# Banded attention with the query and key weights multiplied once

## The reference, cut to what matters

```python
x = x + attn(_layernorm(x))         # the banded attention, changed
x = x + xattn(_layernorm(x), ctx)   # 16 heads over 1601 context rows
x = x + ffn(_layernorm(x))          # 16 heads over itself, then 4 experts

def attn(x, W_qkv, b_qkv, ln_w, ln_b):
    q, k, v = split(x @ W_qkv + b_qkv, 3)
    scores = (q @ k.T) / sqrt(256 * 64)
    scores = scores * band_mask        # keys i-63 .. i, no softmax
    return layer_norm(scores @ v, ln_w, ln_b)
```

## Time and profile before

| | |
|---|---|
| median of 3 runs | 1580.51 us (1579.86 to 1581.3) |
| the profiled execution, its own time | 1582.69 us |
| its span | 1580.8 us |
| PE / DVE / ACT / POOL busy | 1505.1 / 1353.2 / 1256.3 / 192.1 us |
| share of the span | 95% / 86% / 79% / 12% |
| mean granted TensorE clock | 0.989 |

### The profile page before, as it was taken

The page is one execution under the profiler, slowest core; times in us unless marked ns, Lnnn a source line. Parts: engine busy times, 40 slices in busy tenths (PEclk is TensorE's granted clock), DMA queues, the critical chain, the costliest instruction groups (busy, mean ns, idle before and its releaser), DMA issues.

```text
span 1580.8 us, 35391 instructions
## 1 busy us (share of the span) xinstructions
PE 1505.1 (95%) x14142; PEld 626.5 (40%) x14142; DVE 1353.2 (86%) x1914; ACT 1256.3 (79%) x2434; POOL 192.1 (12%) x236
## 2 busy tenths in 40 slices
PE   7977999999999999988999999999999999999997
PEld 6865422222222222346422222222222222338997
DVE  4765999999999999545899999999999999686654
ACT  1136489999999999767469999999999999776654
POOL 3101520000000000000560000000000000003443
PEclk9999999999999999999989999999999999999999
DMA  7000000000000000000003000000000012112111
GB/s 180 0 24 19 1 1 2 2 2 2 2 2 2 2 1 2 2 1 2 0 2 121 2 2 2 2 2 1 2 2 2 2 46 63 28 41 77 56 51 37
DMA packets 34134, 31.19 MB, mean 20 GB/s; under 512 B 10812, under 2 KB 30846, under 8 KB 33982
## 3 DMA queue, kind: packets, MB, share of 16 engines
q1 hardware_dynamic: 31246, 21.99, 4.9%
q0 software_dynamic: 2736, 7.08, 1.5%
HBM read 22.63 MB, written 6.68 MB: 19 GB/s over the span
## 4 chain that ended last, share of the span: by engine, by line
PE 71%; DVE 20%; ACT 6%; issue 2%; DMA 0%; SPq 0%; POOLq 0%; DVEq 0%
PE bank L843 25%; PE bank L830 21%; DVE nm_part L955 15%; PE s_pair L1379 4%; PE bank L1404 4%; PE s_pair L816 4%; PE s_pair L188 2%; ACT p_arena L939 2%; PE s_pair L861 1%; PE bank L627 1%; PE bank L607 1%; ACT o_sb L922 1%; PE bank L869 1%; PE bank L178 1%; PE bank L191 1%
## 5 line engine op out<-in xcount | busy, mean ns | idle before, releaser
L939 ACT ACTIVATE p_arena<-bank 128x512 f32<-128x512 f32 (+1 forms) x1856 | 1003.5, 597 | 67.2 <-PE bank L830 44.8
L955 DVE TENSOR_REDUCE nm_part<-s_pair 128x2 f32<-128x1024 f32 x896 | 1024.6, 1209 | 31.0 <-PE s_pair L816 29.8
L843 PE MATMUL bank<-p_arena,v_aug 128*32 128x256 f32 (+1 forms) x7424 | 596.7, 393 | 13.9 <-ACT o_sb L922 11.7
L816 PE MATMUL s_pair<-x_and_k,q_arena 48*128 48x512 f16 (+1 forms) x2048 | 555.1, 359 | 8.0 <-DVE nm_part L955 6.2
L830 PE MATMUL bank<-q_arena,x_and_k 49*128 49x512 f16 (+1 forms) x1856 | 551.0, 385 | 0.9 <-ACT q_arena L662 0.7
L843 PEld LDWEIGHTS bank<-p_arena,v_aug 128*32 128x32 f32 (+1 forms) x7424 | 147.6, 108 | 387.4 <-ACT p_arena L939 347.6
L830 PEld LDWEIGHTS bank<-q_arena,x_and_k 49*128 49x128 f16 (+1 forms) x1856 | 110.5, 94 | 374.1 <-ACT p_arena L939 331.9
L1031 POOL TENSOR_TENSOR attn_tok<-turned_sums,rden 128x256 f32<-128x256 f32 x30 | 18.6, 620 | 1021.1 <-DVE rden L974 1021.1
L816 PEld LDWEIGHTS s_pair<-x_and_k,q_arena 48*128 48x128 f16 x2048 | 110.7, 94 | 37.2 <-DVE nm_part L955 25.1
L1379 PE MATMUL s_pair<-q_arena 128*128 128x128 f32 x608 | 71.3, 275 | 2.4 <-DVE src_sb L1066 1.8
L1379 PEld LDWEIGHTS s_pair<-q_arena 128*128 128x128 f32 x608 | 70.6, 192 | 3.7 <-DVE src_sb L1066 2.0
(11 more groups left out here) (288 smaller groups left out, 1162.6 us busy)
## 6 DMA issues: line engine op xcount, KB each, us to landing
q_arena<-nm_T SPq DMA_DIRECT2D x512, 0.2 KB
x_and_k<-in_L_ffn_W SPq DMA_DIRECT2D x4, 1024.0 KB, 5.0
v_aug<-in_L_ffn_W SPq DMA_DIRECT2D x8, 512.0 KB, 5.9
res_rows<-x_and_k SPq DMA_DIRECT2D x1, 2048.0 KB, 8.5
x_rows<-src_sb SPq DMA_DIRECT2D x4, 512.0 KB, 3.0
x_and_k<-in_x SPq DMA_DIRECT2D x1, 1536.0 KB, 10.6
p_arena<-in_ctx SPq DMA_DIRECT2D x12, 128.0 KB, 2.0
q_arena<-in_L_attn_W_qkv SPq DMA_DIRECT2D x1, 768.0 KB, 5.3
```

Source lines behind the costliest of these rows:

```text
L816: last = pe.matmul(m_tile[slot % 2][:, part * 512 + place:part * 512 + place + width], q_op[rows, pair, at_q:at_q + P], k_op[rows, pair, k ...
L843: last = pe.matmul(o_bank[32 * a:32 * a + 32, low:low + width], v_aug[0:m, kt, b % 4 * 4 + a, :], at.prob(4 * unit + i)[0:m, low:low + wid ...
L939: act.activation(at.prob(4 * unit + i)[0:m, :], score_bank[k % 3][0:m, :], ACT.Exp, scale=SCALE).then_inc(z["exp"], 1)
L955: dve.tensor_reduce(partials[:, first:second + 1:second - first], banks, AX.X, ALU.max, negate=True).then_inc(z["m_free"], 1)
```

## The change

The change computes Wq Wk^T once, ahead of the first tile, and puts it in the place of the query weights. Rows are then projected to keys alone, and their raw transposed form takes the place of the queries. The bias Wq bk is added to the keys, now by ScalarE in two activations of 128 columns. The term that comes from the query bias depends on the key row alone, so it is computed as a 257th column of the values and added to the scores as a per-row scalar while they are masked, in two operations of 128 columns. `band_v` moves to `p_arena` and grows to 257 columns; `xT` goes. The semaphores `ld_small` and `kept` are merged into `ld_rows` and `res_bias`, so VectorE's wait ahead of the cross attention counts two more loads.

The fold itself (`fold_tensor`, `fold_scalar`, `fold_vector`): eight transposes of the two weight halves, their copies, four products of 256 columns, ten products of one column, and the copies back. TensorE waits for all of it (`fold` at 9) before it turns the first tile.

```diff
-        band_v = carve(q_arena, 3584, 4, C)
+        band_v = carve(p_arena, 512, 4, C + 1)
-        band_rows = carve(q_arena, 7168, 3, C)
+        v_row = q_arena[:, 7168:7168 + C + 1]
+        band_rows = carve(q_arena, 7168 + C + 1, 2, C)
-        xT = carve(p_arena, 512, 2, KC, P)
+        wq_T, wk_T, bq_wide = attn_tok[:, 0:KC, :], attn_tok[:, KC:2 * KC, :], carve(attn_tok[:, 4, :], 0, KC, P)
+        key_bias = attn_tok[:, 5, 0:KC]
...
+        def fold_tensor(pe):
+            pe.wait_ge(s["ld_band"], 16 * 5)
+            for half, b in ((0, 2), (1, 3)):
+                for o in range(KC):
+                    for k in range(KC):
+                        last = pe.transpose(bank(b)[:, o * C + k * P:o * C + (k + 1) * P],
+                                            w_band[:, k, half * C + o * P:half * C + (o + 1) * P], ident[:, :])
+            last.then_inc(s["fold"], 1)
+            pe.wait_ge(s["fold"], 4)
+            pe.wait_ge(s["ld_band"], 16 * 5)
+            for m in range(KC):
+                for o in range(KC):
+                    pe.matmul(bank(4)[:, m * C:(m + 1) * C], wk_T[:, o, m * P:(m + 1) * P], wq_T[:, o, :], start=o == 0, stop=o == KC - 1)
+            for m in range(KC):
+                for o in range(KC):
+                    pe.matmul(bank(5)[:, m:m + 1], wq_T[:, o, m * P:(m + 1) * P], bqk_col[:, KC + o:KC + o + 1], start=o == 0, stop=o == KC - 1)
+            for m in range(KC):
+                for o in range(KC):
+                    pe.matmul(bank(5)[:, KC + m:KC + m + 1], wk_T[:, o, m * P:(m + 1) * P], bqk_col[:, o:o + 1], start=o == 0, stop=o == KC - 1)
+            for o in range(KC):
+                last = pe.matmul(bank(5)[:, 2 * KC:2 * KC + 1], bq_wide[:, o, :], bqk_col[:, KC + o:KC + o + 1], start=o == 0, stop=o == KC - 1)
+            last.then_inc(s["fold"], 1)
+
+        def fold_scalar(act):
+            act.wait_ge(s["fold"], 1)
+            act.activation(wq_T, bank(2).rearrange("p (o c) -> p o c", o=KC), ACT.Copy).then_inc(s["fold"], 1)
+            act.wait_ge(s["fold"], 5)
+            act.activation(w_band[:, :, 0:C], bank(4).rearrange("p (m c) -> p m c", m=KC), ACT.Copy).then_inc(s["fold"], 1)
+
+        def fold_vector(dve):
+            dve.wait_ge(s["fold"], 1)
+            dve.wait_ge(s["ld_band"], 16 * 5)
+            dve.tensor_copy(bq_wide, bqk_col[:, 0:KC].unsqueeze(2).broadcast_to([P, KC, P])).then_inc(s["fold"], 1)
+            dve.tensor_copy(wk_T, bank(3).rearrange("p (o c) -> p o c", o=KC)).then_inc(s["fold"], 1)
+            dve.wait_ge(s["fold"], 5)
+            dve.tensor_copy(key_bias, bank(5)[:, 0:KC]).then_inc(s["fold"], 1)
+            dve.tensor_copy(w_band[:, :, 2 * C - 1:2 * C].rearrange("p k u -> p (k u)"), bank(5)[:, KC:2 * KC]).then_inc(s["fold"], 1)
+            dve.tensor_copy(v_row[:, 0:1], bank(5)[:, 2 * KC:2 * KC + 1]).then_inc(s["fold"], 1)
...
         def band_tensor(pe):
             pe.wait_ge(s["const"], 4)
-            pe.wait_ge(s["ld_band"], 16 * 5)
+            fold_tensor(pe)
             pe.wait_ge(s["band_zero"], 2)
+            pe.wait_ge(s["fold"], 9)
...
                     pe.wait_ge(s["band_st"], i + 1)
+                    pe.wait_ge(s["band_qkv"], i + 1)
...
-                    pe.wait_ge(s["band_qkv"], 2 * i + 2)
+                    pe.wait_ge(s["band_k"], i + 1)
...
-                    for f in range(4):
+                    q, x_T = (r - 1) % 2, band_qk[:, (r - 1) % 4, 0:KC, :]
+                    for f in range(KC):
...
-                        last = pe.matmul(bank(4 + q)[:, 0:C], xT[:, q, k, :], w_band[:, k, 2 * C:3 * C],
+                        last = pe.matmul(bank(4 + q)[:, 0:C + 1], x_T[:, k, :], w_band[:, k, 2 * C - 1:3 * C],
...
                     norm_root(act, r % 2, s["band_ln"], 4 * i, s["band_ln_root"])
+                    if isinstance(i, int) and i == 0:
+                        fold_scalar(act)
                     act.wait_ge(s["band_xT_ps"], i + 1)
-                    if some(i - 1):
-                        act.wait_ge(s["band_qkv_ps"], i - 1)
-                    act.activation(xT[:, r % 2, :, :], bank(r % 2)[:, 0:C].rearrange("p (k t) -> p k t", k=KC),
+                    act.activation(band_qk[:, r % 4, 0:KC, :], bank(r % 2)[:, 0:C].rearrange("p (k t) -> p k t", k=KC),
                                    ACT.Copy).then_inc(s["band_xT"], 1)
+
+                if (i := tile_at(t, 1, NT)) is not None:
+                    act.wait_ge(s["band_qkv_ps"], i + 1)
+                    if isinstance(i, int) and i == 0:
+                        act.wait_ge(s["fold"], 9)
+                    for f in range(KC):
+                        last = act.activation(band_qk[:, (r - 1) % 4, KC + f, :], bank(2 + (r - 1) % 2)[:, f * P:(f + 1) * P],
+                                              ACT.Identity, bias=key_bias[:, f:f + 1])
+                    last.then_inc(s["band_k"], 1)
...
-                    dve.tensor_tensor(band_st[:, (r - 2) % 2, :], bank(6)[:, 0:2 * P], band_mask[:, :],
-                                      ALU.mult).then_inc(s["band_st"], 1)
+                    dve.wait_ge(s["band_qkv"], i + 1)
+                    for h, keys in ((0, (r - 2) % 4), (1, (r - 3) % 4)):
+                        half = slice(h * P, (h + 1) * P)
+                        last = dve.scalar_tensor_tensor(band_st[:, (r - 2) % 2, half], bank(6)[:, half], band_v[:, keys, 0:1],
+                                                        band_mask[:, half], ALU.add, ALU.mult)
+                    last.then_inc(s["band_st"], 1)
...
                     norm_apply(dve, i, r % 2, x_sb[:, i, :], xin[:, r % 2, :], s["band_ln"], 4 * i, s["band_ln_root"])
+                    if isinstance(i, int) and i == 0:
+                        fold_vector(dve)
...
-                    dve.tensor_tensor(band_qk[:, q, :, :], bank(2 + q % 2).rearrange("p (f t) -> p f t", f=4),
-                                      bqk_col[:, :].unsqueeze(2).broadcast_to([P, 4, P]), ALU.add).then_inc(s["band_qkv"], 1)
-                    dve.tensor_tensor(band_v[:, q, :], bank(4 + q % 2)[:, 0:C], band_rows[:, 0, :],
-                                      ALU.add).then_inc(s["band_qkv"], 1)
+                    if isinstance(i, int) and i == 0:
+                        dve.wait_ge(s["fold"], 9)
+                    dve.tensor_tensor(band_v[:, q, :], bank(4 + q % 2)[:, 0:C + 1], v_row, ALU.add).then_inc(s["band_qkv"], 1)
...
-            dve.wait_ge(s["ld_rows"], 16 * len(ROWS))
+            dve.wait_ge(s["ld_rows"], 16 * (len(ROWS) + 2))
```

More of the change, by code:

```diff
@@ L108, in decoder_layer_kernel @@
                  "band_av", "band_out", "band_root", "band_ln_root", "band_xb", "xw_ps", "xw", "v_const", "k_const", "q_const",
-                 "ld_small", "res_bias", "kept")
+                 "res_bias", "band_k", "fold")
         x_view = io["x"][0].rearrange("(t p) c -> p t c", p=P)
@@ L167, in tick @@
                     q, prev = (r - 3) % 4, (r - 4) % 4
-                    pe.matmul(bank(7)[:, 0:C], band_st[:, q % 2, 0:P], band_v[:, q, :], start=True, stop=False)
-                    pe.matmul(bank(7)[:, 0:C], band_st[:, q % 2, P:2 * P], band_v[:, prev, :],
+                    pe.matmul(bank(7)[:, 0:C], band_st[:, q % 2, 0:P], band_v[:, q, 1:C + 1], start=True, stop=False)
+                    pe.matmul(bank(7)[:, 0:C], band_st[:, q % 2, P:2 * P], band_v[:, prev, 1:C + 1],
                               start=False, stop=True).then_inc(s["band_av"], 1)
                 if (i := tile_at(t, 2, NT)) is not None:
-                    pe.wait_ge(s["band_qkv"], 2 * i + 2)
+                    pe.wait_ge(s["band_k"], i + 1)
                     if some(i):
@@ L183, in tick @@
                     if some(i - 1):
-                        pe.wait_ge(s["band_qkv"], 2 * (i - 1))
-                    q = (r - 1) % 2
-                    for f in range(4):
+                        pe.wait_ge(s["band_k"], i - 1)
+                        pe.wait_ge(s["band_qkv"], i - 1)
+                    q, x_T = (r - 1) % 2, band_qk[:, (r - 1) % 4, 0:KC, :]
+                    for f in range(KC):
                         for k in range(KC):
-                            pe.matmul(bank(2 + q)[:, f * P:(f + 1) * P], w_band[:, k, f * P:(f + 1) * P], xT[:, q, k, :],
+                            pe.matmul(bank(2 + q)[:, f * P:(f + 1) * P], w_band[:, k, f * P:(f + 1) * P], x_T[:, k, :],
                                       start=k == 0, stop=k == KC - 1)
                     for k in range(KC):
-                        last = pe.matmul(bank(4 + q)[:, 0:C], xT[:, q, k, :], w_band[:, k, 2 * C:3 * C],
+                        last = pe.matmul(bank(4 + q)[:, 0:C + 1], x_T[:, k, :], w_band[:, k, 2 * C - 1:3 * C],
                                          start=k == 0, stop=k == KC - 1)
@@ L251, in tick @@
                     ring, c = 2 + q3, 5 * i
-                    dve.scalar_tensor_tensor(band_tmp[:, q3, :], o, mean_var[:, ring, 0:1], band_rows[:, 1, :],
```

(22 more changed lines are left out.)

## The result

The changed kernel takes 1590.62 us in the median of 6 runs (1589.09 to 1600.28), the kernel before 1579.75 us in the median of 6 (1579.03 to 1581.3). The ratio is 1.0069, 95% interval 1.0039 to 1.0098: slower by 10.9 us.

The account below looks back on a forecast made before the run. TensorE was taken as full in the banded stage, with VectorE's ring at most some 0.2 us shorter. Terms 6.9 - 0.3 + 4.6 - 1.1 + 0.2 = +10.3 us on the median 1580.51 gave 1590.8 us, range 1584.0 to 1598.0.

Parts of the forecast that it names:

- TensorE no longer the bound: Banded stage, each tick: dropped products save TensorE 0.89 us, leaving 4.03 of 4.925, and the saving turns into idle time.
- The masking's two halves, +0.20: VectorE's masking in each tick: two 128-column operations in place of one add 0.20 us, bounds +0.08 and +0.25.
- The keys behind the copy: ScalarE, each tick: keys wait behind the next tile's copy; the value product's cover is short by 0.1 to 0.25 us.
- The new ring, 5.28: Banded stage, scores to next scores through VectorE, transpose, copy and keys: 5.28 us against 4.925; thirteen periods add 4.6 us.
- The fold and the start, 6.9: Kernel start: the fold ahead of everything makes first scores 6.9 us later, 4.4 to 10, at about 24 us.
- half of a low clock: First projections after the fold: a low clock would cost 1.8 us more, of which half, 0.9, was counted.
- First period and last: Ends of the banded stage: first period 4.64 us, -0.3; last 3.85 us, -1.1.
- The sum: Whole kernel: start 6.9, first period -0.3, thirteen periods 4.6, last period -1.1, last masking 0.2, together +10.3 us.
- clock fell in the loop: Rival, banded loop: TensorE, busy 76%, drops to 1.2 GHz, +40 us or more, some 1630; chance 0.03.
- table for Identity: Rival, ScalarE in each tick: Identity forces two function table loads, 2.56 us, +41 us, 1630; chance 0.02.
- ring was not short enough to hide the change: Rival, banded stage: keys hide behind the value product, ring 4.80 us, total 1582, no measurable change; chance 0.08.
- nor was TensorE the bound: Rival, banded stage: TensorE stays the bound, pace 4.03 us, the saving is real, -5.9 us, 1575; chance 0.07.

Follow-up runs that it names:

- both orders: Changed kernel with ScalarE's key activations ahead of its copy and VectorE normalising the input tile before its wait for the scores: 1577.47 us, ratio 0.9982.
- the four variants above: Changed kernel with whole masking, keys ahead of the copy, VectorE's order alone, or both orders: 1593.46, 1588.95, 1578.57 and 1577.47 us.
- the keys first: Changed kernel with ScalarE's two key activations ahead of its copy of the next tile's transposed rows: 1588.95 us in one run.
- VectorE's order alone: Changed kernel with VectorE normalising the input tile before its wait for the scores, and ScalarE's input root first: 1578.57 us in one run.
- the early fold: Changed kernel with both orders, its fold waiting only for the weights and bias column, not the three broadcast rows: 1573.38 us, ratio 0.9963.
- the whole masking: Changed kernel with masking as one 256-column product, leaving the query bias term out of the scores: 1593.46 us in one run.
- the last two versions: The changed kernel with both orders, and the one with the early fold: 1577.47 and 1573.38 us.

## Why the prediction was right

The mechanism was right: the fold ahead of everything, a ring that the dropped products don't shorten, and the waits that they turn into. The time, 1590.6 us against a forecast of 1590.8, is closer than its terms deserve, and that is luck: the ring was taken 1.0 us too long and the start 1.7 too short, and the median of the kernel before came out 0.8 us under the 1580.51 that the forecast was added to. By its steps:

- **TensorE no longer the bound.** Right. It would need 4.03 us a tick; with both orders the pace is 4.07, and with the given ones 5.20. It was busy for 54.46 of 66.69 us, 82%, where I had three quarters.
- **The masking's two halves, +0.20.** 37.23 to 37.76 us is 0.53, where it was 0.34: +0.19. The experiment gave 0.18.
- **The keys behind the copy.** Right as a wait, seen twelve times. Copy start to weight load is 40.20 to 41.15, 0.95, where I had 0.98. Taken out, it gave 0.24 per period in most, within my 0.1 to 0.25, but 0.20 in the mean, and 0.06 once VectorE's order was changed.
- **The new ring, 5.28.** It is 5.18, 5.20 in the mean. The step that I over-sized is the end of L155 to the copy's start: 39.67 to 40.20 is 0.53, and I took 0.65 from ticks in which the copy came 0.67 and 0.68 after it. My lower bound had 0.54. The thirteen periods added 3.6 us, not 4.6.
- **The fold and the start, 6.9.** It is 8.6, the term that I under-sized. The first transpose came at 20.54 us, not 19.4: the loads ended 0.5 later, and from the first thin record to the end of the last (17.07 to 19.81) it took 2.7 us, not 2.2. The transposes, copies and four products were right within 0.2 (3.57 us from the products' start to the first thin record, where I had 3.5). Then I counted half of a low clock, and it was low in full: the changed kernel's table by stretches, length, busy by engine, granted clock, has

```profile
21.00:25.00 4.00, 3.57 (x13) 3.18 (x14) 0.58 (x2) 0.56 (x2) 0.64 (x1) 0.57 1.01 123
```

  a granted clock of 0.57, mostly the 1.2 GHz level. Eight records took 2.07 us there, and 1.06 later. This term is one execution's: with the same fold, first scores came between 25.71 and 27.68 us in the four variants above that wait for the same loads.
- **First period and last.** 4.49 (forecast 4.64) and 3.93 (3.85). From the last scores to the last value product it took 3.3 us, 0.3 more than before, where I had 0.2.
- **The sum.** 8.6 - 0.4 + 3.6 - 1.0 + 0.3 = +11.1 against +10.3. The trace has the last value product at 105.60 us, where it was 94.59: +11.0.
- **The rivals.** No clock fell in the loop: from 30.79 to 97.48 us the granted clock was 1.00. ScalarE loaded no table for Identity: the ticks have no such record. The Trainium skill, ScalarE: Activation LUTs, section Table sets, puts identity in every set; by that rule no load was due, and the trace agrees, with two key activations in 0.62 us beside the square roots. The ring was not short enough to hide the change, nor was TensorE the bound.

Shown by runs: the fold's 9.8 us at the first scores, the masking's 0.18, the keys' 0.24, VectorE's ring as the holder of the pace, and that the saving becomes real once VectorE's order is changed. Not settled: why the kernel without the fold is 4.3 us above the kernel before in the median when its stage ends 0.9 us late. The 3.6 us that the profiled execution loses after the cross attention's start lie within the 4.6 us by which single executions differ there. The profile before has a granted clock of 0.95 from 760 to 860 us, the changed one 1.00 and the one without the fold 0.93, so the clock at the joint between the two attentions is one thing that differs each time. That it explains either difference is not shown.

## What to carry to other kernels

Before you take work from the engine that is full, time the next ring of waits around it, from a result to the wait that it feeds one tick later. Here it stood some 0.2 us behind in 4.9 (the 4.92 us with the keys first, less 0.18 for the longer masking, is 4.74), so a saving of 0.9 us per tick could pay at most that until VectorE's order was changed. Look where each new instruction stands in its engine's fixed order, since an evacuation behind a copy inherits the copy's wait. A fold of weights is serial work at the slowest moment of the kernel; it is repaid only by what the loop can then save, so let it wait for its own loads alone.

## What the runs showed of the hardware that was not expected

- One-column float32 products cost as much as those of 128 columns. In the changed kernel eight of their records take 0.90 us from start to next start (18.33 to 19.23), and eight of 128 columns 0.89 (36.97 to 37.86): 0.11 us per record. In the version with both orders, where the fold is slow to its end, eight take 1.71 us (18.26 to 19.97), 0.21 each.
- In one and the same fold TensorE became fast at different points. In the changed kernel, with VectorE's order alone and with the early fold, the middle eight one-column records took 1.03 us; with both orders, with the keys first and with the whole masking they took 1.84 or 1.85. In the first three, records were slow again right after the wait for the copies back (8 in 2.07 us), and there the granted clock fell to 0.50. No run shows what decides it.
- The granted clock of the profile reads 1.00 throughout the start of every profile, until its first fall, even where records take twice their later time: without the fold, eight records of the first projections take 2.08 us at 11.35 us, and 1.06 later. There the length of the records tells more than the clock column.
- Runs spread more wherever the changed stage is in the kernel: 11.2 us in the changed kernel (6 runs), 11.1 without the fold (10), 11.9 and 9.4 in the last two versions (12 and 10), against 2.3, 2.3 and 7.1 in the kernel before (6, 13 and 27) and 5.4 with its order changed (11). In the changed kernel the mean granted clock went with it: 0.992 in the shortest and 0.983 in the longest. Why is open.
